# A two-layer transformer on one core: slot orders of three attention stages changed, start-up loads spread over the first stage

## The chip, the cores and the metric

The kernel runs on one core of a Trainium2 chip. The time is the device time of one execution in microseconds (us). TensorE (PE in the profile, PEld for its weight loads), VectorE (DVE), ScalarE (ACT), GpSimd (POOL) and SyncE (SP) run their own instruction streams and wait for each other by semaphores alone.

## The reference

`x` is 8 images of 256 tokens by 256 channels, float32. Eight sublayers run one after the other, each as `x = x + f(layernorm(x))`:

1. softmax attention, 16 heads of 16 channels (in the kernel: stage `attn_a0`, index A0S)
2. a linear layer with a scale per output row and a bias (`ffn0`, F1)
3. softmax attention over 4 wide heads of 64 channels, with biases (`attn_b0`, B0)
4. the linear layer of 2 again (`ffn0`, F3)
5. retention: scores times a decay mask `exp(-s*(t-k))`, two RMS norms, weights quantised to -1, 0, 1 (`ret1`, R1)
6. a gated feed-forward layer with a Hadamard transform (`ffn1`, F5)
7. differential attention **between the heads of one token**: 32 by 32 scores for each token, softmax, first half minus lambda times second half (`attn_b1`, B1)
8. the feed-forward layer of 6 again (`ffn1`, F7)

Matrix products of activations with weights are made to float32 precision from a high and a low part of each factor (three products); the retention's weights are exact in one part.

## The kernel before

All of `x` stays in SBUF. A stage handles one image in 8 slots of a global slot counter; `due(g, offset)` (L390) says that a step of image `b` falls in slot `8b + offset` of its stage. `together` (L420) walks the slots from -24 on and, in each, calls every stage's `at_slot(g)` on each engine. So each engine has one fixed order of instructions, written by hand: first by slot, then by stage, then by the order of the lines in that stage's `at_slot`. An engine that waits holds all that stands behind it. B0 begins at slot 76, F3 at 92, R1 at 148, F5 at 212, B1 at 276 and F7 at 338 (`START`, L417); F1 runs inside the slots of A0S. The stages overlap at their ends.

**Start (L470 to L495, L736 to L742, L881 to L889, L1240 to L1249, L2342 to L2344).** SP issues all input loads in one run: image 0 of `x`, the four `a0` weights, the identity matrix, small constants, images 1 to 7, more constants, the first raw weights (`f0`, `b0_q`, 1 MB of `w1`), the retention weights; only then does it reach the stage loops. Every progress semaphore begins at 1 rather than 0, so that a wait on image -1 passes: ACT increments each of them in a loop (L883 to L885), and DVE, POOL, SP and PE wait for `primed`, the last increment. POOL first fills constant rows of three K buffers, DVE fills four V buffers, and DVE splits all four `a0` weights into their low parts (`low_a0`) after the statistics of image 0. The one load semaphore of images 1 to 7 is waited for as a whole.

**Q and K in A0S and R1** go to DRAM (`store`, L506; four DMAs an image) and come back rearranged (`load_q`, `load_k`, L519 and L531; eight each). `pa` and `pb` are PSUM banks that x, Q, K and V outputs share.

**B0, one image (L2099 to L2121 on PE, L1501 to L1536 on DVE).** Slots 0 and 2: scores; DVE takes their maxima in 1 and 3. Slot 3: PE turns the next x and makes V (`v_out`, offset -5) into `pb`. Slot 4 on DVE: `x_low`, then `heads_out` of the second half (L1482: a reciprocal, a product), then far down the list `v_out` (L1461), which empties `pb`. Slot 4 on PE: `max_turned` (L2044) writes `pb`, and so waits for that `v_out`. Then K, the linear layer, transposed scores, `y_out`, Q.

**R1 (L1945 to L1967 on PE, L1379 to L1404 on DVE).** `k_out` of a later image stands in slot 5 (offset -11) and writes `pa`; it waits for `normed` of image b-3 (L1817), which DVE's `heads_out` of the second half makes in the same slot.

**B1 (L2204 to L2226 on PE, L1602 to L1622 on DVE, L1131 to L1157 on ACT).** Per image: `scores` of halves 0 and 1 (slots 0 and 1); DVE `less_maximum` (clamp, maximum, subtract; L1569), ACT `probs` (exp), DVE `weights_of` (sum, reciprocal, product; L1578), PE `turned` (slot 8), ACT `turned` (slot 8), PE `attend` (slot 9), ACT `heads_out` and `store_out` to DRAM, SP `load_out`, POOL `clipped`, ACT `squares`, DVE `square_sums` (slot 13), POOL `token_heads`, PE `a_turned` (18), `y_out` and DVE `residual` (24). PE's slot 0 holds, in order, `y_out` of image b-3, both `turned` of b-1, `x_turned` of b+2, and `scores(b, 0)`. ACT's slot 0 begins with `turned` of b-1.

Of the kernel before, what the change touches and what calls it, by code (L numbers as in the profile page):

```python
# [25 lines left out]
F32 = mybir.dt.float32  # L26
F32R = mybir.dt.float32r
ALU = mybir.AluOpType
# [3 lines left out]
P = 128  # L32
B = 8
# [104 lines left out]
class Signals:  # L138


    def __init__(self, ctx, nc):
# [4 lines left out]
        self.base, total = [], {k: 1 for k in names}  # L146
# [7 lines left out]
def build(nc, T, out):  # L154
    ctx = ExitStack()
    with ctx:
# [158 lines left out]
        x0_in, x_in, first_in, const_in = sem("x0_in"), sem("x_in"), sem("first_in"), sem("const_in")  # L315
        a0_in, a0_high, a0_low = sem("a0_in"), sem("a0_high"), sem("a0_low")
        negs_done, ones_done, k_ready, had_done = sem("negs_done"), sem("ones_done"), sem("k_ready"), sem("had_done")
        primed = sem("primed")
# [28 lines left out]
        A0 = ("a0_q", "a0_k", "a0_v", "a0_o")  # L347
        a0_raw = {n: prob_bufs[k // 2][:, k % 2 * 512:k % 2 * 512 + 512].rearrange("p (t n) -> p t n", t=CT) for k, n in enumerate(A0)}

        def split_done(eng, name):  # L350

            if name == "attn_a0":
                eng.wait_ge(a0_low, len(A0))
                return
            eng.wait_ge(w_split, ORDER.index(NEEDS[name]) + 1)


        def in_stage(eng, s, i):
# [10 lines left out]
            def prev(name, alone=apart):  # L369
                if name in per:  # L370
# [96 lines left out]
        n_const = 16 * (3 + 4 + 6 + 4)  # L467
# [3 lines left out]
        def _(sp):  # L471

            for b in range(B):
                sp.dma_start(x[:, b, :].rearrange("p (t c) -> p t c", t=TT),
                             T["hidden"][b].rearrange("(t p) c -> p t c", p=P)).then_inc(x_in if b else x0_in, 16)
                if b == 0:
                    for n in A0:
                        sp.dma_start(a0_raw[n], T[n].rearrange("(t p) n -> p t n", p=P)).then_inc(a0_in, 16)
                    for dst, src in ((ident[:], T["ident"]), (negs[:], T["r1_s"].rearrange("(a n) -> a n", a=1).to_broadcast([P, 16])),
                                     (diff[:], T["diff"])):  # L480
                        sp.dma_start(dst, src).then_inc(first_in, 16)
            for dst, src in ((caus[:], T["caus"]), (had_raw[:], T["had"]), (sel_raw, T["sel"])):
                sp.dma_start(dst, src).then_inc(const_in, 16)
            for dst, n in ((bq, "b0_bq"), (bk, "b0_bk"), (qkvn, "r1_qkvn"), (projn, "r1_projn")):
                sp.dma_start(dst[:], T[n]).then_inc(const_in, 16)
            for dst, n in ((bv[:], "b0_bv"), (bo0[:], "b0_bo"), (bo1[:], "b1_bo"), (bf[:], "f0_b"), (swb, "f0_s"), (nwb[:], "r1_nw")):
                sp.dma_start(dst, T[n].rearrange("(a n) -> a n", a=1).to_broadcast([P, C])).then_inc(const_in, 16)
# [1964 lines left out]
```

## Time and profile before

| | us |
|---|---|
| median of 3 runs | 1123.61 |
| the 3 runs | 1122.81, 1123.61, 1127.87 |
| the profiled execution | 1126.71 |
| its span, first to last instruction | 1124.9 |
| mean granted TensorE clock | 0.896 of full speed |

A row of the timeline gives the start in us from the span's start, the time, engine, line, operation, what is written from what, the count; in brackets the engine's idle time before it and what ended that. `SPq` and `ACTq` are DMA issues. A row of the waits gives total us, times, longest. In `--windows` rows the columns are the stretch, its length, and busy us (and instructions) of PE, PEld, DVE, ACT, POOL, then PE clock, DMA share and GB/s.

### The profile page before, as it was taken

What the parts mean: (1) busy time and instruction counts of PE and PEld (TensorE: products, weight loads), DVE (VectorE), ACT (ScalarE), POOL (GpSimd) and SP (SyncE); (2) the same over time, 40 slices, a digit from 0 to 9 for tenths busy, and PEclk for the clock granted to TensorE, in tenths of its full rate; (3) what the DMA queues carried; (4) which work ended last, traced back from release to release, by engine and by line L of the source; (5) the groups of instructions that cost most, each with busy time, mean ns of one, the idle gap of its engine ahead of it and who ended that gap; (6) DMA issues with size and microseconds to landing.
All of it is one profiled execution on the core that took longest, in us unless ns stands there. A gap on an engine that the chain in (4) does not pass through costs nothing.

```text
span 1124.9 us, 21059 instructions
## 1 busy us (share of the span) xinstructions
PE 915.9 (81%) x8018; PEld 776.4 (69%) x8018; DVE 695.5 (62%) x1291; ACT 367.3 (33%) x663; POOL 317.2 (28%) x352
## 2 busy tenths in 40 slices
PE   3589988787777678778877999997678874799998
PEld 2466665566666566656656999995566653799997
DVE  4468777646665567887775554536766767454443
ACT  2136554444222222233434332233222321332332
POOL 4202222224568474211111112100154443330000
PEclk9779998898898989898888999999777887899999
DMA  8745541001100002455440000022454445100000
GB/s 227 232 139 157 147 119 55 12 11 38 48 20 1 1 1 66 131 152 163 120 123 1 2 1 1 1 57 51 82 113 85 86 90 82 33 15 20 10 20 20
DMA packets 148580, 76.78 MB, mean 68 GB/s; under 512 B 108992, under 2 KB 139712, under 8 KB 148480
## 3 DMA queue, kind: packets, MB, share of 16 engines
q1 hardware_dynamic: 139376, 65.47, 23.1%
q0 software_dynamic: 1424, 4.98, 1.5%
q10 hardware_dynamic: 7680, 4.98, 1.5%
q8 instruction: 64, 1.05, 0.4%
q14 instruction: 36, 0.29, 0.1%
HBM read 45.77 MB, written 29.36 MB: 67 GB/s over the span
## 4 chain that ended last, share of the span: by engine, by line
PE 58%; DVE 26%; issue 7%; ACT 4%; SPq 2%; DMA 1%; POOL 1%; ACTq 0%; DVEq 0%; POOLq 0%
PE SC L380 17%; PE pb L380 8%; PE OT L380 8%; PE pa L380 4%; DVE mx L1315 3%; PE OT L2173 3%; PE OT L1890 3%; DVE OS L1488 2%; PE SC L1843 2%; PE SC L1872 2%; PE OT L2088 2%; PE SC L2161 2%; DVE pr L1576 2%; PE pa L2356 2%; DVE m L1574 2%
## 5 line engine op out<-in xcount | busy, mean ns | idle before, releaser
L380 PE MATMUL SC<-xT_h,w_h 128*128 128x256 f32 x512 | 148.3, 290 | 13.8 <-DVE xT_l L1737 11.5
L380 PE MATMUL SC<-xT_l,w_h 128*128 128x256 f32 x512 | 146.4, 286 | 0.0
L380 PE MATMUL SC<-xT_h,w_l 128*128 128x256 f32 x512 | 145.7, 285 | 0.0
L380 PEld LDWEIGHTS SC<-xT_h,w_h 128*128 128x128 f32 x512 | 98.4, 192 | 17.0 <-DVE xT_l L1737 15.1
L380 PE MATMUL OT<-w,Qs 128*128 128x256 f32 x768 | 102.9, 283 | 2.2 <-DVE Qs L1747 1.4
L1315 DVE TENSOR_REDUCE mx<-SC 128x4 f32<-128x1024 f32 x64 | 78.1, 1220 | 42.0 <-PE SC L1843 41.6
L380 PEld LDWEIGHTS SC<-xT_h,w_l 128*128 128x128 f32 x512 | 98.5, 192 | 0.0
L380 PEld LDWEIGHTS SC<-xT_l,w_h 128*128 128x128 f32 x512 | 98.2, 192 | 0.0
L380 PEld LDWEIGHTS OT<-w,Qs 128*128 128x128 f32 x768 | 95.1, 189 | 4.2 <-issue 2.6
L1743 DVE TENSOR_TENSOR hidden_f<-SC,silu_gate 128x512 f32<-128x512 f32 x64 | 44.1, 689 | 85.5 <-ACT silu_gate L1199 85.5
L1747 DVE TENSOR_TENSOR Qs<-hidden_f,Qs 128x512 fp32r<-128x512 f32 x64 | 45.2, 707 | 44.7 <-ACT Qs L1207 44.7
L1199 ACT ACTIVATE silu_gate<-SC 128x512 f32<-128x512 f32 x64 | 38.2, 597 | 101.5 <-PE SC L380 98.9
L749 POOL TENSOR_SCALAR ve<-mv 128x2 f32<-128x2 f32 x32 | 7.1, 221 | 191.3 <-DVE mv L1268 112.5
L1207 ACT ACTIVATE Qs<-hidden_f 128x512 fp32r<-128x512 f32 x64 | 40.4, 632 | 50.4 <-DVE hidden_f L1743 49.6
L2356 PE MATMUL pa<-ident,xn 128*128 128x128 f32 x192 | 34.0, 306 | 26.7 <-DVE xn L1291 20.3
L943 ACT ACTIVATE a_pr<-SC 128x1024 f32<-128x1024 f32 x32 | 32.8, 1026 | 49.2 <-PE SC L1872 49.2
L2356 PEld LDWEIGHTS pa<-ident,xn 128*128 128x128 f32 x192 | 24.4, 158 | 32.7 <-issue 21.3
L865 POOL TENSOR_SCALAR g_ve<-g_mv 128x2 f32<-128x2 f32 x16 | 3.9, 242 | 149.3 <-DVE g_mv L1722 148.8
L778 POOL TENSOR_TENSOR hr<-ssqe,half_pow 128x32 f32<-128x32 f32 x8 | 44.3, 5536 | 1.5 <-POOL ssqe L776 1.5
L943 ACT ACTIVATE pr<-SC 128x1024 f32<-128x1024 f32 x32 | 32.8, 1024 | 33.0 <-PE SC L1872 32.9
L764 POOL TENSOR_TENSOR x<-x,bo 128x512 f32<-128x512 f32 x16 | 20.4, 1273 | 67.9 <-DVE xn L1448 50.5
L1332 DVE TENSOR_TENSOR pr<-SC,mask 128x512 f32<-128x512 f32 x43 | 29.4, 685 | 16.2 <-PE SC L1872 15.9
(424 smaller groups left out, 2592.2 us busy)
## 6 DMA issues: line engine op xcount, KB each, us to landing
Qs<-q_stack SPq DMA_DIRECT2D x56, 128.0 KB, 2.8
k_stack<-KT_h SPq DMA_DIRECT2D x16, 256.0 KB, 2.4
k_stack<-KT_l SPq DMA_DIRECT2D x16, 256.0 KB, 3.1
q_stack<-QT_h SPq DMA_DIRECT2D x16, 256.0 KB, 2.2
q_stack<-QT_l SPq DMA_DIRECT2D x16, 256.0 KB, 2.8
o_groups<-b_O ACTq DMA_DIRECT2D x8, 512.0 KB, 3.0
Qs<-q_stack SPq DMA_DIRECT2D x56, 64.0 KB, 2.9
Ks<-k_stack SPq DMA_DIRECT2D x28, 128.0 KB, 3.0
```

Of the source, the lines that this page charges most:

```text
L380: ins = pe.matmul(out_ap, left[a], right[b], start=first and n == 0, stop=last and n == len(terms) - 1, **more)
L778: pool.tensor_tensor(hr0[:], ssqe[:], half_pow[:], ALU.pow).then_inc(sig.sem["hpow"], 1)
L943: act.activation(pr[(b * ROUNDS + r) % len(pr)][:], SC[1][:], ACT.Exp, scale=st.scale).then_inc(sig.sem["probs"], 1)
L1199: act.activation(silu_gate[:], SC[r % 2][:, 0:512], ACT.Silu).then_inc(sig.sem["g_silu"], 1)
L1207: act.activation(joined(hid[r % 2][0][:]), hidden_f[:], ACT.Copy).then_inc(sig.sem["g_hh"], 1)
L1315: dve.tensor_reduce(mx[:, t, m0:m0 + 16].rearrange("p (u g) -> p u g", u=2)[:, :, 2 * k:2 * k + 2], SC[0][:].rearrange("p (u g k) -> p u g ...
L1332: dve.tensor_tensor(to[:, :, 0, :], of[:, :, 0, :], heads, ALU.mult)
L1743: dve.tensor_tensor(hidden_f[:], SC[r % 2][:, 512:1024], silu_gate[:], ALU.mult).then_inc(sig.sem["g_hid"], 1)
L1747: dve.tensor_tensor(joined(hid[r % 2][1][:]), hidden_f[:], joined(hid[r % 2][0][:]).bitcast(F32), ALU.subtract)\
L1890: ins = pe.matmul(OT[0][32 * n:32 * n + 32, t0:S], Vr[b % len(Vr)][:, kt, 2 * r + u, :], p[:, u, kt, t0:S], start=kt == 0, stop=kt == 1, t ...
L2173: ins = pe.matmul(OT[0][:, 256 * h + 64 * n:256 * h + 64 * n + 64], b1_P[h][:, u, 8 * n:8 * n + 8, :].rearrange("p g b -> p (g b)"), own_h ...
L2356: ins = pe.transpose(ps[:, c * S + t * P:c * S + t * P + P], src[:, t, c * P:c * P + P], ident[:])
```

## The change

Six groups of edits, cut below to what matters.

- Semaphores count from 0, and a wait for 0 is left out; ACT's loop and `primed` go. ACT loads its function table with a small copy instead, then takes each `a0` weight as it lands.
- Each input has a semaphore of its own. SP first loads image 0, `a0_k`, the identity, `a0_q`, image 1, `a0_v`, image 2, `a0_o`. The other images and constants and weights are issued inside A0S's slots -2 to 50. The K fills are spread over POOL's slots, the four V fills stand behind `normalise` of images 0 and 1 on DVE, and `low_a0` is cut in two.
- The scale of `f0` has a semaphore of its own.
- B0: `v_out` of images 4 to 7 one slot earlier on PE, before `x_turned`; DVE's `v_out` right behind `maximum`; second `heads_out` and `a_low` one slot later.
- R1: K one slot later on all engines; `x_high` first in ACT's slot; `a_low` behind `masked` and `x_low`.
- B1: both `scores` first in slot 0; both `less_maximum` in slot 0; `weights_of` in slots 1 and 2; `probs` in 0 and 1, ahead of all else on ACT in slot 0, then `load_k` (six DMAs), then `turned`; `x_low` one slot later.

```diff
-        self.base, total = [], {k: 1 for k in names}
+        self.base, total = [], {k: 0 for k in names}
...
 # SP
+            X_LOADS = {-2: 3, 4: 4, 12: 5, 20: 6, 28: 7}
+            LATER = {1: 4, 3: 0, 5: 1, 6: 2, 7: 3, 11: 5, 36: 6, 44: 7, 46: 8, 48: 9, 50: 10}
+            load_x(0)
+            load_a0("a0_k")
+            sp.dma_start(ident[:], T["ident"]).then_inc(ident_in, 16)
+            load_a0("a0_q")
+            load_x(1)
+            load_a0("a0_v")
+            load_x(2)
+            load_a0("a0_o")
...
+                                if g in X_LOADS:
+                                    load_x(X_LOADS[g])
+                                if g in LATER:
+                                    load_later(LATER[g])
...
 # SP, ret1
-                                for b in due(g, -10):
+                                for b in due(g, -9):
                                     store(b, "kl", "kstore", "kload", KT, k_dram)
...
 # SP, attn_b1
+                            for b in due(g, -8):
+                                load_q(b)
                             for b in due(g, -7):
                                 load_k(b)
                             for b in due(g, 9):
                                 load_out(b)
-                            for b in due(g, -7):
-                                load_q(b)
...
 # POOL
+            clear_stack(0)
...
+                        if g in (-21, -13):
+                            clear_stack((g + 29) // 8)
...
 # ACT
-            for signal in sig.sem.values():
-                act.sem_inc(signal, 1)
-            act.sem_inc(primed, 1)
-
-            act.wait_ge(a0_in, 16 * len(A0))
+            act.wait_ge(ones_done, 1)
+            act.activation(silu_first[:], ones[:, 0:1], ACT.Copy)
             for n in A0:
+                act.wait_ge(a0_in[n], 16)
                 act.activation(W[n][0][:], a0_raw[n], ACT.Copy).then_inc(a0_high, 1)
...
 # ACT, attn_b1
+                    for b in due(g, 0):
+                        probs(b, 0)
+                    for b in due(g, -8):
+                        load_k(b)
                     for b in due(g, 8):
                         turned(b)
+                    for b in due(g, -16):
+                        high(b, x_pair(s, b), pa, "xT", "vp", 1, "xh")
+                    for b in due(g, 1):
+                        probs(b, 1)
                     for h in range(TT):
                         for b in due(g, 9):
                             heads_out(b, h)
-                    for b in due(g, 1):
-                        probs(b, 0)
                     for b in due(g, 9):
                         store_out(b)
...
 # DVE
+                    if s == 0 and b == 0:
+                        low_a0(1)
+                    if s == 0 and b < 2:
+                        for v in V_rings["attn_a0"][2 * b:2 * b + 2]:
+                            dve.memset(v[:], 1.0).then_inc(ones_done, 1)
...
 # DVE, attn_b0
+                    for b in due(g, -5):
+                        if b >= 4:
+                            v_out(b)
+                    for b in due(g, -4):
+                        if b < 4:
+                            v_out(b)
                     for b in due(g, 5):
                         max_low(b)
                     for b in due(g, -12):
                         x_low(b)
                     for c in range(CT):
-                        for b in due(g, 10 + 2 * c):
+                        for b in due(g, 10 + 3 * c):
                             heads_out(b, c)
-                    for b in due(g, 13):
+                    for b in due(g, 14):
                         a_low(b)
...
 # DVE, attn_b1
+                    for h in range(TT):
+                        for b in due(g, 0):
+                            less_maximum(b, h)
                     for b in due(g, 24):
                         residual(b)
-                    for b in due(g, -16):
+                    for b in due(g, 1):
+                        weights_of(b, 0)
+                    for b in due(g, -15):
                         low(b, x_pair(s, b), pa, "xh", "xl")
-                    for b in due(g, 1):
-                        less_maximum(b, 0)
                     for b in due(g, 2):
-                        weights_of(b, 0)
-                        less_maximum(b, 1)
+                        weights_of(b, 1)
...
-                    for b in due(g, 4):
-                        weights_of(b, 1)
...
 # PE, ret1
-                        for b in due(g, -11):
+                        for b in due(g, -10):
                             k_out(b)
...
 # PE, attn_b0
+                    for b in due(g, -6):
+                        if b >= 4:
+                            v_out(b)
                     for b in due(g, -13):
                         x_turned(b)
...
 # PE, attn_b1
+                    for h in range(TT):
+                        for b in due(g, 0):
+                            scores(b, h)
                     for b in due(g, 24):
                         y_out(b)
...
-                    for h in range(TT):
-                        for b in due(g, h):
-                            scores(b, h)
```

## Rows read from the trace of the kernel before

**Rows 1.** The page: the chain that ended last, by engine

```profile
PE 58%; DVE 26%; issue 7%; ACT 4%; SPq 2%; DMA 1%; POOL 1%; ACTq 0%; DVEq 0%; POOLq 0%
```

**Rows 2.** Windows: the start, B0, R1 and B1 in turn

```profile
0.00:40.30 40.30, 14.88 (x84) 13.37 (x84) 15.25 (x33) 8.63 (x14) 14.64 (x18) 0.96 0.82 235
...
250.00:429.00 179.00, 137.22 (x1192) 115.86 (x1186) 114.52 (x214) 45.91 (x85) 108.03 (x90) 0.90 0.05 17
...
465.00:600.00 135.00, 106.07 (x1048) 78.69 (x1048) 105.00 (x265) 48.26 (x137) 24.05 (x51) 0.87 0.45 131
...
769.00:968.00 199.00, 141.51 (x1292) 109.84 (x1291) 137.18 (x178) 53.48 (x78) 68.61 (x57) 0.78 0.45 81
```

**Rows 3.** Timeline of the start

```profile
0.91 3.65 POOL L738 MEMSET Ks<- 32x2048 f32 x2
1.15 0.91 DVE L1242 MEMSET V<- 128x1024 f32 x1 [0.16 <-issue]
...
8.55 0.75 DVE L1265 BATCH_NORM_STATS2 bst<-x 128x6 f32<-128x256 f32 x2 [3.27 <-ACTq L885]
...
17.79 0.58 PE L380 MATMUL pa<-xT_h,a_k_h 128*128 128x256 f32 x1 [1.41 <-DVE xT_l L1302]
...
24.34 0.55 SPq L512 DMA_DIRECT2D k_stack<-KT_h  x1
...
40.34 0.51 PE L1843 MATMUL SC<-Ks,Qs 48*128 48x256 f32 x4 [1.80 <-DMA Ks<-k_stack]
```

**Rows 4.** Issue to landing: all x loads, then all Q and K stores

```profile
DMA to landing us min/median/max: 2.8/5.2/6.7
...
DMA to landing us min/median/max: 2.1/2.8/7.9
```

**Rows 5.** Timeline of one B0 image

```profile
367.11 1.75 DVE L1488 RECIPROCAL OS<-OT 128x256 f32<-128x256 f32 x1
368.89 0.42 DVE L1490 TENSOR_TENSOR ON<-OT,OS 128x256 f32<-128x256 f32 x1
369.24 0.68 DVE L1466 TENSOR_TENSOR V<-pb,bv 128x512 f32<-128x512 f32 x1
...
370.06 0.66 PE L2050 MATMUL pb<-ident,sq 128*128 128x128 f32 x2 [4.28 <-DVE V L1466]
...
371.69 0.86 DVE L1494 TENSOR_TENSOR aT_l<-ON,aT_h 128x512 fp32r<-128x512 f32 x1
```

**Rows 6.** Waits in B0, 250 to 430 us

```profile
PE pb L2050 <- DVE V L1466: 17.2, 4, 4.4
...
PE pb L2050 <- DVE Vw L1466: 8.5, 3, 4.3
```

**Rows 7.** Waits in R1, 465 to 600 us

```profile
PE pa L380 <- DVE ON L1343: 5.5, 3, 2.3
...
PE pa L380 <- DVE scratch L1343: 3.9, 2, 2.3
```

**Rows 8.** Windows: the seven distances of DVE's first maximum in B1, together

```profile
sum 171.55, PE 128.25 PEld 101.53 DVE 119.78 ACT 45.56 POOL 58.30; mean PE 18.32 PEld 14.50 DVE 17.11 ACT 6.51 POOL 8.33
```

**Rows 9.** Timeline of one B1 image, and of the stage's end

```profile
848.35 1.92 PE L2188 MATMUL OT<-scratch,b_DT 128*32 128x128 f32 x64
...
852.37 1.06 ACT L1102 ACTIVATE pr<-pr 128x1024 f32<-128x1024 f32 x1 [1.43 <-DVE pr L1576]
...
854.10 2.19 ACTq L305 DMA_DIRECT2D b_KD<-k_tokens  x6
...
862.22 0.63 ACT L1116 ACTIVATE sq<-ON 128x512 f32<-128x512 f32 x1 [0.39 <-POOL ON L794]
...
864.68 3.51 PE L2173 MATMUL OT<-ident,V 128*128 128x64 f32 x16
...
944.47 1.23 DVE L1572 TENSOR_SCALAR pr<-SC 128x1024 f32<-128x1024 f32 x1 [3.07 <-PE SC L2161]
...
963.37 0.58 PE L380 MATMUL SC<-xT_h,w_h 128*128 128x256 f32 x1 [11.53 <-DVE xT_l L1737]
```

More of the change, by code:

```diff
@@ L369, in prev @@
             def prev(name, alone=apart):
-                if name in per:
+                if name in per and i * per[name] + base[name] > 0:
                     eng.wait_ge(sig.sem[name], i * per[name] + base[name])
@@ L471, in _, with load_x @@
         def _(sp):
-            for b in range(B):
+            def load_x(b):
                 sp.dma_start(x[:, b, :].rearrange("p (t c) -> p t c", t=TT),
[L475 to L481, printed above, removed]
@@ L1380, in at_slot @@
                     if ret:
-                        for b in due(g, 26):
-                            a_low(b)
                         for b, r in running(g, 0):
@@ L1386, in at_slot @@
                             x_low(b)
+                        for b in due(g, 26):
+                            a_low(b)
                         for b in due(g, -12):
                             low(b, QT, pb, "qh", "ql")
-                        for b in due(g, -10):
+                        for b in due(g, -9):
                             low(b, KT, pa, "kh", "kl")
@@ L1519, in at_slot @@
                         low(b, b0_Q, pb, "qh", bq, "ql")
-                    for b in due(g, -4):
-                        v_out(b)
                     for b in due(g, -21):
@@ L1808, in q_out @@
                     wait("al", b - 5, 1)
+                    if s == A0S and b == 0:
+                        pe.wait_ge(a0_low, 2)
                     if ret and b == 0:
@@ L1815, in k_out @@
                     wait("xl", b, 1)
+                    if s == A0S and b == 0:
+                        pe.wait_ge(a0_low, 1)
                     if ret:
@@ L1821, in v_out @@
                     wait("ql", b, 1)
+                    if s == A0S and b == 0:
+                        pe.wait_ge(a0_low, 3)
                     if s == A0S and b >= 6:
@@ L1963, in at_slot @@
                             q_out(b)
-                        for b in due(g, -11):
+                        for b in due(g, -10):
                             k_out(b)
@@ L2119, in at_slot @@
                     for b in due(g, -5):
-                        v_out(b)
+                        if b < 4:
+                            v_out(b)
                 return at_slot
```

105 lines of the change are left out of this document (57 added, 48 removed).

## The prediction

> **What bounds the kernel now.** First the page's chain: PE carries 58% of the chain that ended last and DVE 26% [rows 1], so most of the time PE works or DVE does while PE waits. Then the windows by stage [rows 2]: the feed-forward stages and the body of A0S, whose order the change leaves, are not among them; in the four stretches shown PE is busy for 37% of the start, 77% of B0, 79% of R1 and 71% of B1, and DVE for 38%, 64%, 78% and 69%. No engine is full there. The time goes into hand-overs within one fixed order per engine, so an edit of the order can move it. The reader should see in each of the next rows one such hand-over: an engine's idle time in brackets, and who ended it.
>
> **Start.** DVE has image 0 in SBUF 2.8 us after its issue at 0.7 (the shortest landing of its load [rows 4]), that is at 3.5, and begins its statistics at 8.55, released by ACT's loop of semaphore increments [rows 3]. That is 5.0 us of pure waiting, which counting from zero removes. What is late next: DVE must split the weights as they land (the last of them is issued at about 4.2, lands by the median of 5.2 us [rows 4] at 9.4, and two steps of the 128x512 kind, 0.63 us on ACT [rows 9] and put at 0.7 on DVE, split it by 10.7), and then two V fills stand ahead of `x_low` of image 0, each 0.91 us and a 0.16 gap [rows 3], 2.1 us, and `x_low` itself, 0.7. So the first K product starts at about 13.5 instead of 17.79 [rows 3]: 4.3 us. The K store now follows that product by 6.5 us (24.34 less 17.79), of which I estimate 2 us as SP still issuing loads (the product, two evictions and the issue make up the rest); that part goes too. The Q and K stores of image 0 then stand behind megabytes of weights: the slowest takes 7.9 us to land where the median of all is 2.8 [rows 4], 5.1 us more. Sum: 4.3 + 2 + 5.1 = 11. Given back: image 3 of `x` is now issued only in slot -2 behind the K fetch, and DVE's statistics of it stand in slot 1, in front of score maxima: I estimate 2 us from the landing time of 2.8 us; the second pair of V fills stands ahead of Q's low part of image 0, 1 us. **Term: -8 us**, ends -5 (only the removed loop) and -11.
>
> Costed at nothing: the K fills, now spread over POOL's slots (3.65 us each [rows 3], POOL being busy for 14.6 of the first 40.3 us [rows 2]; without that cover each would put 3.65 us ahead of a `rstd`); the table load, now under the first x load; the 31 later loads on SP, at about 0.45 us of issue each (a K store's took 0.55 [rows 3]) 14 us over 50 slots of more than 2 us, where SP mostly waits for PE and DVE (without that cover, see the third rival); the semaphore of `f0`'s scale, whose consumer is POOL slots later.
>
> **B0.** PE stands still before `max_turned` seven times, 17.2 + 8.5 = 25.7 us [rows 6]. Rows 5 show why: `pb` holds V until DVE's `v_out`, which waits its turn behind `x_low`, a 1.75 us reciprocal and a 0.42 us product, while PE idles 4.28 us. The change puts `v_out` ahead of these. The 2.2 us of reciprocal and product go one slot later, behind `max_low`; then `y_out` waits for them, for ACT's high part (0.6, as its square of that shape [rows 9]) and for `a_low` (0.86 [rows 5]). By the order of the slots PE meanwhile has the transposed max, K, the linear layer's turn and transposed scores to do, so I let about 1.1 us an image come back as a wait of `y_out`: 25.7 less 7 times 1.1. **Term: -18 us**, ends -10 (more comes back) and -26 (nothing does).
>
> **R1.** `k_out` waits in its slot for DVE's second `heads_out`: 5.5 + 3.9 = 9.4 us in five images [rows 7]. One slot later that work is done. But K then stands next to V in PE's order, in slots 6 and 7, and K's store and its fetch are one slot closer (3 us to land against two slots of 2 us). About half is kept. **Term: -5 us**, ends 0 and -9.
>
> **B1.** The seven distances between images are 171.55 us, 24.5 each, with 17.1 of DVE work in each [rows 8]. Now DVE ends an image's weights, PE turns both halves (3.51 us the first [rows 9]), turns an x, and only then makes the scores for which DVE waits (3.07 us idle at 944.47 [rows 9]). With `scores` first in PE's slot that wait goes. The next wait to end last is a longer one: on ACT, `turned` of image b-1 stands behind `probs(b, 0)` and six K issues. From DVE's first clamp T: clamp, maximum and subtract at 1.23 each (the clamp's row) 3.7, exp 1.06, six issues 2.19, an eviction 0.6 as the square of that shape [rows 9]: PE attends at T + 7.6. From there to the end of the squares now takes 14.5 us (848.35 to 862.85 [rows 9]: evictions, DRAM round trip, clip), 1.5 of it a queue on ACT that goes, so the squares end at T + 20.6. DVE's `square_sums` waits for them, then one `normalise`: the next T is 22 later, or a little more when PE runs at its lower level. I take 22.5 to 23 for six distances and 18.5 for the first, which has no such partner: 155 instead of 171.55. At the end 963.37 - 944.47 = 18.9 us pass from the last T to the feed-forward stage's first product [rows 9]; that product stands behind the squares of image 6, whose attend now falls about at T, so that they end some 15 us after it, and then 20.6: 5 to 6 are lost. **Term: 155 - 171.5 + 6 = -10 us**, ends -20 (distance 21.5, about DVE's 17.1 and its own waits) and +12 (26.5, with PE at the lower level and the ring as it stands).
>
> **Sum:** -8 - 18 - 5 - 10 = -41 us. The profiled execution took 1126.7 us, 1.8 over its span, which gives 1085.7; it stood 3.1 above the median of the runs, so a median of 1082.6, **1083 us**.
>
> **Rivals.** *B1 gives nothing* (0.15). For it: the round trip above is as long as the whole present distance, less 2 us. Against it: DVE's own work is 17.1 [rows 8], and part of the trip runs beside it. 1093 us.
>
> *B0 moves its wait* (0.12). PE's idle before `max_turned` goes, and the same time stands before `y_out`, because `heads_out`, ACT's high part and `a_low` are now the last link. For it: this chain is 2.2 + 0.6 + 0.9 us [rows 5, 9], nearly the 4.28 that goes. Against it: PE has work of about that length in between. 1101 us.
>
> *The loads in rounds push Q and K back* (0.08). Behind a run of weights the slowest store took 7.9 instead of 2.8 us [rows 4]; the loads left for the rounds are about 5.2 MB, at the 235 GB/s of the start [rows 2] 22 us of transfer, and if each one holds Q or K by its own length where PE waits for them, -8 becomes +14: 1105 us. The rows of a quiet queue speak against it: a Q or K fetch has a slot or more of slack. The Trainium skill ("DMA: Bandwidth & Descriptors", section "Queues, rings and completion order") says that each DMA engine consumes the descriptors of one issuer's ring in order; by that rule the rounds' loads delay whatever SP issues behind them, which would be this rival. The 7.9 us row agrees with the rule; whether PE then waits no run here shows.
>
> *Slower: DVE stands at `square_sums`* (0.07). Place: B1, DVE's slot 5. If the attend of image b-1 slips not only behind ACT's `probs` and issues but behind both of PE's turns at the lower clock level (7 us, by 3.51 a half [rows 9]), T to squares grows from 20.6 to some 28, and the distance to 30. Price: 7 times 5.5 is 39 us. It decides from a distance of 29 on (24.5 plus the other 31 us over seven). Then 1131 us.
>
> **How the numbers follow.** The forecast itself, all four terms with their sign, has 0.58. A change under 0.5% (5.6 us, about what a measurement of this kernel tells from none) needs two of the rivals together. Faster by more: the forecast, and nearly all of the first three rivals, 0.88; same 0.05; slower 0.07. The range: the terms' ends sum to -66 and +7; all at one end is unlikely, so it runs from 1060, nearly the lower sum, to 1112, past the third rival, and leaves out the fourth and the extremes.
>
> **What would show it.** In the changed profile: statistics at 3.5 us; first score product near 31 us instead of 40.34; no PE wait on DVE's V before `max_turned`, at most 1 to 2 us before `y_out`, and B0 some 18 us shorter; no `pa` wait on `heads_out` in R1; in B1 clamps 22 to 23 us apart, DVE idle before `square_sums`, not before the clamp. Wrong would be: clamps over 25 apart, a Q or K fetch ending PE's waits in the first stage, or `y_out` waiting 4 us in B0.

## The result and the profile after

The changed kernel takes 1091.83 us (median of 4 runs, 1081.66 to 1093.77), the kernel before 1123.21 in the same comparison: a ratio of 0.9697, 95% interval 0.9628 to 0.9766, so 3.0% less. (The ratio, here and below, is taken over the runs; the two medians alone give 0.9721.) Ratios are of fast runs alone, which leaves out one run of e1 below (2039.78 us), one of e9 (1088.25 us), and two or three runs of the kernel before beside e5 to e8 and beside e12 (1136.72 to 1143.41 us). The profiled execution took 1093.38 us with a span of 1091.6.

Marks in the two traces tell where the time went. A stage's mark is the start of an instruction that each image has once or in a known number: DVE's first score maximum (A0S, B0), its first masked product (R1), its first maximum of the clamped scores (B1, 1.25 us behind the first clamp, so with the same distances). R1 ends with its last masked product, F5 with its last SiLU. Marks are rounded to 0.1 us.

| stretch, us | before | after | difference | forecast |
|---|---|---|---|---|
| span's start to A0S's first maximum | 40.9 | 36.3 | -4.6 | -11 of the start term |
| A0S, first to last image | 145.4 | 154.6 | +9.2 | +3 of the start term |
| A0S's last to B0's first | 66.0 | 62.1 | -3.9 | 0 |
| B0, first to last image | 173.9 | 157.3 | -16.6 | -18 |
| B0's last to R1's first | 38.2 | 43.8 | +5.6 | 0 |
| R1, first image to its end | 136.1 | 131.2 | -4.9 | -5 |
| F5's end to B1's first | 8.8 | 4.5 | -4.3 | 0 |
| B1, first to last image | 171.6 | 155.0 | -16.6 | -16.5 |
| B1's last to F7's first SiLU | 22.4 | 24.9 | +2.5 | +6 |

The distances of B0 and B1 and R1's stretch came out within 2 us of their numbers. The start did not: up to the first maximum it gains less than half of what was forecast, and the distances from image 0 to image 2 then lose almost twice that (8.5 of the 9.2 us; the table of first maxima below has them).

The page's part 4 of the changed kernel, the chain that ended last by engine, is to be read against [rows 1]. PE and DVE have shrunk, and DMA has grown from 1% to 5%. By line, 4 of these 5% are the two legs of B1's trip through DRAM (`DMA o_groups<-b_O` 2%, `DMA ON<-o_groups` 2%).

```profile
PE 52%; DVE 23%; issue 8%; DMA 5%; ACT 4%; SPq 3%; POOL 3%; ACTq 1%; POOLq 0%; DVEq 0%
```

**The start.** The timeline of the changed kernel (start, busy us, engine, line, tiles, in brackets the idle time before and who ended it):

```profile
3.46 0.75 DVE L1293 BATCH_NORM_STATS2 bst<-x 128x6 f32<-128x256 f32 x2 [2.47 <-DMA x<-in_hidden]
...
6.48 3.69 POOL L765 MEMSET a_K<- 32x2048 f32 x2 [0.15 <-POOL rstd L778]
7.53 2.79 DVE L1319 TENSOR_SCALAR xn<-x,mv,rstd 128x256 f32<-128x256 f32 x2
...
11.96 0.91 DVE L1325 MEMSET V<- 128x1024 f32 x1 [0.16 <-issue]
13.04 0.91 DVE L1325 MEMSET a_V<- 128x1024 f32 x1 [0.16 <-issue]
...
14.55 0.58 PE L380 MATMUL pa<-xT_h,a_k_h 128*128 128x256 f32 x1 [3.00 <-DVE xT_l L1335]
...
18.75 2.28 DVE L1319 TENSOR_SCALAR xn<-x,mv,rstd 128x256 f32<-128x256 f32 x2
18.93 0.37 SPq L533 DMA_DIRECT2D k_stack<-KT_h  x1
...
21.20 0.91 DVE L1325 MEMSET a_V<- 128x1024 f32 x1 [0.16 <-issue]
22.27 0.91 DVE L1325 MEMSET a_V<- 128x1024 f32 x1 [0.16 <-issue]
23.82 0.36 SPq L533 DMA_DIRECT2D q_stack<-QT_h  x1
...
35.72 0.51 PE L1886 MATMUL SC<-Ks,Qs 48*128 48x256 f32 x4
```

Statistics begin at 3.46 and the first K product at 14.55, close to the forecast (3.5 and 13.5). But DVE normalises image 0 in 2.79 us and image 1 in 2.28, while POOL fills a K stack (L765), and between K's store (18.93) and Q's (23.82) lie 4.9 us, in which DVE does that slow pair and two V fills. So the first score product is at 35.72 instead of the forecast 31.

Behind it, two waits of the changed kernel, from the waits of PE and of DVE (34 to 108 us; columns: us in total, times, longest), neither of which the kernel before has:

```profile
PE SC L1915 <- DMA Qs<-MT_l: 3.5, 1, 3.5
```
```profile
DVE bst L1293 <- DMA x<-in_hidden: 3.1, 1, 3.1
```

DVE stands 3.1 us for image 3 of `x`; at PE the transposed scores stand 3.5 us for the maxima's rows. The view of the fetch line, 63 to 73 us, shows the queue in which those rows travel: the fetches of image 2 take 6.8 us to land, where the median of the line over the whole trace is 3.0. They were issued right behind nine constant loads (59.1 to 63.4 us).

```profile
DMA to landing us min/median/max: 3.8/6.8/6.9
```

These waits are not the whole loss. The windows from image 1's first maximum to image 2's, before and after (PE busy and count first; the granted clock is the number after POOL's):

```profile
62.20:81.90 19.70, 15.14 (x112) 11.30 (x110) 13.25 (x18) 6.36 (x10) 0.94 (x2) 0.74 0.44 136
```
```profile
59.30:85.80 26.50, 19.12 (x110) 14.56 (x110) 13.36 (x18) 6.93 (x11) 0.94 (x2) 0.62 0.73 154
```

Nearly the same products take PE 4 us longer at a lower granted clock, so more of this stretch ran at the lower of TensorE's two levels (1.2 and 2.4 GHz). What part of the 6.8 us that costs the image, and whether the waits are what lowers the clock, no run here separates.

**B0.** PE's waits, 250 to 412 us, against [rows 6]:

```profile
PE pb L380 <- DVE aT_l L1527: 10.9, 6, 3.1
...
PE pb L2095 <- DVE Vw L1499: 2.3, 1, 2.3
PE pb L2095 <- DVE V L1499: 1.9, 3, 0.9
```

The 25.7 us before `max_turned` (there L2050, here L2095) are 4.2. The new wait is the one named beforehand, `y_out` for `aT_l`: 1.8 us in each of six images where I let 1.1 come back.

**R1.** PE's waits, 452 to 585 us, against [rows 7]: no `pa` wait on `heads_out` is left. PE waits longer for DVE's masked products instead, 18.1 us by two lines where the same view of the kernel before (465 to 600 us, shown first) has 11.6: 6.5 of the 9.4 us come back there, somewhat more than the half of the forecast. By the mark the stage is 4.9 us shorter. One trace doesn't fix the size: in the ten traces here with this order the stretch takes from 124.3 to 131.2 us, in the four without it (before, e2, e3, e4) from 133.5 to 136.1.

```profile
PE OT L1890 <- DVE pr L1333: 7.7, 11, 1.5
...
PE OT L1890 <- DVE r_pr L1333: 3.9, 6, 1.0
```
```profile
PE OT L1933 <- DVE pr L1366: 12.3, 13, 1.6
PE OT L1933 <- DVE r_pr L1366: 5.8, 7, 1.4
```

**B1.** DVE's longest wait before (769 to 968 us), then its waits after (753 to 934 us) and the windows of the seven distances together, against [rows 8]:

```profile
DVE pr L1572 <- PE SC L2161: 19.1, 8, 7.1
```
```profile
DVE ssq L1632 <- ACT sq L1147: 33.1, 7, 6.4
DVE xn L1593 <- POOL rstd L778: 5.9, 5, 1.3
DVE pr L1609 <- PE SC L2210: 2.1, 1, 2.1
```
```profile
sum 155.00, PE 116.39 PEld 92.83 DVE 114.60 ACT 45.81 POOL 57.85; mean PE 16.63 PEld 13.26 DVE 16.37 ACT 6.54 POOL 8.26
```

DVE's wait for scores falls from 19.1 to 2.1 us; it now waits in every image for the squares. The distances are 22.1 us in the mean, with 16.4 of DVE's own work. The round trip has the length of the forecast: the sums of squares below start 20.7 us behind the clamp at 863.38, where the forecast had T + 20.6, and the next clamp follows at 884.72.

```profile
884.12 0.69 DVE L1632 TENSOR_REDUCE ssq<-sq 128x32 f32<-128x512 f32 x1 [5.41 <-ACT sq L1147]
```

### The profile page after: what moved, and what is told of

Same layout as the page of the kernel before. It is cut to its first block, busy times and chain, and to the rows that moved or that the text cites. A ratio compares the mean times of both kernels' runs of the same rounds, so it can differ in the third digit from the quotient of the medians.

```text
span 1091.6 us, 20960 instructions
## 1 busy us (share of the span) xinstructions
PE 902.0 (83%) x8018; PEld 766.6 (70%) x8018; DVE 695.2 (64%) x1291; ACT 367.4 (34%) x664; POOL 320.3 (29%) x352
## 4 chain that ended last, share of the span: by engine, by line
PE 52%; DVE 23%; issue 8%; DMA 5%; ACT 4%; SPq 3%; POOL 3%; ACTq 1%; POOLq 0%; DVEq 0%
PE SC L380 17%; PE pb L380 8%; PE OT L380 8%; PE pa L380 3%; PE OT L1933 3%; DVE mx L1348 3%; PE SC L1915 2%; DVE OS L1521 2%; DMA ON<-o_groups 2%; PE OT L2237 2%; PE OT L2133 2%; PE SC L1886 2%; DMA o_groups<-b_O 2%; PE pa L2404 1%; SPq L644 1%
## 5 line engine op out<-in xcount | busy, mean ns | idle before, releaser
L1230 ACT ACTIVATE silu_gate<-SC 128x512 f32<-128x512 f32 x64 | 38.2, 597 | 96.9 <-PE SC L380 96.4
L2237 PE MATMUL OT<-scratch,b_DT 128*32 128x128 f32 x512 | 24.8, 375 | 29.4 <-ACT b_DT L1138 29.4
L2404 PE MATMUL pa<-ident,xn 128*128 128x128 f32 x192 | 32.7, 297 | 17.6 <-DVE xn L1319 13.0
L2237 PEld LDWEIGHTS OT<-scratch,b_DT 128*32 128x32 f32 x512 | 22.4, 155 | 30.8 <-issue 30.7
```

The source lines that it names most:

```text
L1230: act.activation(silu_gate[:], SC[r % 2][:, 0:512], ACT.Silu).then_inc(sig.sem["g_silu"], 1)
L2237: ins = pe.matmul(OT[h][32 * i:32 * i + 32, P * n:P * n + P], b1_DT[:, 4 * h + n, a0:a0 + 32], b1_VB[:, 8 * i + 4 * h + n].rearrange("p e ...
L2404: ins = pe.transpose(ps[:, c * S + t * P:c * S + t * P + P], src[:, t, c * P:c * P + P], ident[:])
```

## Experiments

The theory after the result: the three orders do what was forecast, and the changed start does not, for causes of its own. The kernel before measures 1123 us in the first comparison and 1129 to 1137 on the later chips, so kernels are compared by their ratio to it.

### One part at a time

e1 is the kernel before with the three changed orders, e2 with the changed start alone, e3 and e4 with B0's and B1's order alone. Each takes the hunks of the diff above that belong to its part, for example all of e3 on DVE:

```diff
+                    for b in due(g, -5):
+                        if b >= 4:
+                            v_out(b)
+                    for b in due(g, -4):
+                        if b < 4:
+                            v_out(b)
...
-                        for b in due(g, 10 + 2 * c):
+                        for b in due(g, 10 + 3 * c):
...
-                    for b in due(g, 13):
+                    for b in due(g, 14):
                         a_low(b)
...
-                    for b in due(g, -4):
-                        v_out(b)
```

> Kernel before with the changed orders of B0, R1 and B1, and its own start. Theory A (the start term failed: by the stage marks of the two traces the changed start gains 4.6 us up to the first score maximum and gives back 9.2 over images 0 to 2): 1123 - 38 = 1085 us, some 5 us below the changed kernel's 1092. Rival B (the start is worth its -8 and one of the orders brought less than its stage marks say): 1100 us. By the spread of the runs so far (12 us in the changed kernel) a difference of 5 us is at the edge of what can be told.

> Kernel before with the changed start alone (counts from zero, a semaphore per input, loads in rounds). Theory A: 1123 + 4.6 = 1128 us; the first score maximum near 36.3 us instead of 40.9, the last of the stage near 191 instead of 186. Rival B: 1115 us, the last maximum of the stage near 178.

> Kernel before with the changed order of B0 alone. Theory A (the seven distances shrink by 16.6 and the 5.6 us that were lost between B0's last maximum and R1's first mask come from R1's order): 1106 us. Rival B (those 5.6 us are B0's own, work that its last images push behind them): 1112 us.

> Kernel before with the changed order of B1 alone. Theory A (seven distances -16.6, lead-in -4.3, tail +2.5): 1123 - 18.4 = 1105 us, clamps 22 us apart with DVE waiting at square_sums. Rival B (part of that is the earlier stages' doing, the clock level that they leave): 1111 us or more.

| kernel | ratio to before | 95% interval |
|---|---|---|
| e1, three orders | 0.9634 | 0.9601 to 0.9666 |
| e2, start | 1.0008 | 0.9977 to 1.0039 |
| e3, B0 | 0.9836 | 0.9805 to 0.9868 |
| e4, B1 | 0.9833 | 0.9803 to 0.9862 |

Of 1128.7 us (the kernel before in this set) B0's order takes 18.5 and B1's 18.8; what is left of e1's 41.3 us, 4, would be R1's, less than the intervals of the three ratios can tell from nothing (R1's order wasn't run alone). e1 and e4 come out as their theories A, reckoned from 1128.7: 1087.1 us against 1091, and 1109.0 against 1110, with rivals at 1106 and 1117. e3 falls between its two cases as worded in us, but those were reckoned from 1123; from 1128.7, A means 1111 and B 1117, and 1109.7 speaks for A on the time. In its trace, though, B0's last maximum to R1's first mask is 42.9 us against 38.2, so 4.7 of the 5.6 us do come with B0's order; its distances shrink by 18.2 and R1 behind it by 2.6, and from B0's first maximum to R1's end the trace is 16.1 us shorter.

The start alone is worth nothing: neither A's +4.6 nor B's -8 is in the time. Its marks are A's all the same (first maximum 36.2, last 190.6). But of the 4.3 us by which the stage ends late, 2 are the spread of single traces: e1, e3 and e4, which keep the start of the kernel before, end it at 188.1 to 188.3 and not at 186.3. The rest is made up behind it, by image 2 of B0 (301.6 against 301.7 before). The windows of e2 from A0S's last maximum to B0's first and on to its third show how (PE busy and count first, then the other engines; the granted clock is the number after POOL's):

```profile
190.60:254.10 63.50, 49.82 (x464) 34.70 (x461) 38.40 (x91) 30.78 (x49) 19.91 (x26) 0.92 0.06 15
254.10:301.60 47.50, 36.39 (x318) 32.12 (x318) 30.95 (x59) 17.20 (x36) 25.61 (x21) 0.89 0.09 28
```

and the same of e4, whose code up to B1 is that of the kernel before:

```profile
188.30:252.80 64.50, 51.95 (x464) 35.87 (x463) 38.44 (x90) 30.78 (x49) 19.72 (x25) 0.88 0.05 14
252.80:303.40 50.60, 39.49 (x319) 34.66 (x319) 31.02 (x60) 17.33 (x36) 25.74 (x21) 0.83 0.09 27
```

The same 464 instructions of the first window take PE 49.8 us at a granted clock of 0.92 and 52.0 at 0.88. PE ran at its upper level (2.4 GHz) for more of this stretch in e2. One profile of each doesn't settle whether the changed start brings that about, but other traces speak for executions that differ: from A0S's last maximum to B0's first, e4 takes 64.5 us where the kernel before, the same code up to there, takes 66.1, and e10 takes 66.2 where e8, again the same code up to there, takes 62.1. So the -3.9 us of that row in the table of marks need not be a gain of the change. What is measured is the sum, nothing.

### What the start lost

e5, e6 and e7 each mend one suspect of the changed kernel:

```diff
-                    item(pool, A0S, "rstd", n - 1, 1)
+                    item(pool, A0S, "xn", n - 1, TT)
```
```diff
-            X_LOADS = {-2: 3, 4: 4, 12: 5, 20: 6, 28: 7}
+            X_LOADS = {-2: 4, 4: 5, 12: 6, 20: 7}
...
             load_a0("a0_o")
+            load_x(3)
```
```diff
-            LATER = {1: 4, 3: 0, 5: 1, 6: 2, 7: 3, 11: 5, 36: 6, 44: 7, 46: 8, 48: 9, 50: 10}
+            LATER = {1: 4, 11: 5, 13: 0, 15: 1, 17: 2, 19: 3, 36: 6, 44: 7, 46: 8, 48: 9, 50: 10}
```

> Changed kernel; POOL fills the K stacks of images 1 and 2 after DVE has normalised image 0 and 1, instead of beside it. Theory A (a pair of 128x256 tensor_scalar on DVE stands still while POOL's fill runs): the pairs take 0.73 us each instead of 2.79 and 2.28, the first score maximum is at 33 to 34 us instead of 36.3, the stage's last at 187 to 189 instead of 190.9. Rival B (the pair is slow for another reason, the loads that write x at that time): it still takes over 2 us, nothing moves.

> Changed kernel; image 3 of x is loaded ahead of the slots and each later image one round earlier. Theory A: DVE's wait of 3.09 us for image 3 and PE's 2.84 behind it go; the distance from image 0's first maximum to image 1's is 20 us instead of 23.0, the last maximum of the stage 2 to 3 us earlier (188). Rival B (256 KB more ahead of image 0's K and Q stores): the first maximum is over 1 us later, the last where it was.

> Changed kernel; the four groups of constants move from slots 3 to 7 to slots 13 to 19. Theory A (the Q and K fetches of images 1 and 2 stand behind them on SP and in its DMA queue): fetches land in about 3 us instead of 6.8, the distances of the first two images fall from 23.0 and 26.5 us to 20 or 21 each, the last maximum of the stage 6 to 8 us earlier, 183 to 185. Rival B (they hold up whatever is behind them, wherever they are): the first two distances fall, and the third to fifth grow from 17.6, 19.3 and 22.9 by as much; the last maximum stays at 190. Rival C (the low granted clock of these images, 0.62 to 0.70, makes them long): no distance falls by more than 1 us.

> Changed kernel with the three edits (fills after normalise, image 3 early, constants in slots 13 to 19) and the V fills two slots later, where DVE waits for ACT. Theory A: first maximum near 31 us, last of the stage near 177, and the time by 10 us or more below the changed kernel's, 1078 to 1082 us by the runs so far. Rival B (what the start loses or gains up to here is taken back by the stages behind it, as with the changed start alone, whose last maximum was 4.3 us late and whose time was the same): the last maximum is early, and the time within 4 us of the kernel before with the changed orders alone, 1083 to 1089.

First maxima of the eight images in A0S, by the traces:

| kernel | first | distances | last | ratio to before (interval) |
|---|---|---|---|---|
| before | 40.9 | 21.4, 19.7, 17.6, 19.3, 22.9, 22.4, 22.2 | 186.3 | 1 |
| changed | 36.3 | 23.1, 26.5, 17.6, 19.3, 22.9, 22.4, 22.9 | 190.9 | 0.9697 (0.9628 to 0.9766) |
| e5, fills after normalise | 33.4 | 23.4, 26.5, 17.6, 19.3, 22.9, 22.4, 22.8 | 188.3 | 0.9651 (0.9576 to 0.9725) |
| e6, image 3 early | 36.6 | 21.6, 24.9, 17.6, 19.3, 22.8, 22.4, 22.8 | 188.0 | 0.9618 (0.9556 to 0.9679) |
| e7, constants in slots 13 to 19 | 35.9 | 23.2, 23.4, 17.6, 23.4, 22.9, 22.4, 24.0 | 192.9 | 0.9705 (0.9639 to 0.9771) |
| e8, all three and the V fills | 27.8 | 18.0, 19.7, 19.3, 25.1, 22.9, 22.4, 23.0 | 178.2 | 0.9563 (0.9508 to 0.9618) |

The ratios of e5, e6 and e7 don't differ from the changed kernel's clear of their intervals, so these three are judged by rows and marks alone.

**e5** settles its question. Its timeline, against that of the changed kernel above:

```profile
7.72 0.73 DVE L1319 TENSOR_SCALAR xn<-x,mv,rstd 128x256 f32<-128x256 f32 x2
8.61 3.65 POOL L765 MEMSET a_K<- 32x2048 f32 x2 [2.29 <-DVE xn L1319]
...
17.73 0.73 DVE L1319 TENSOR_SCALAR xn<-x,mv,rstd 128x256 f32<-128x256 f32 x2
18.61 3.66 POOL L765 MEMSET a_K<- 32x2048 f32 x2 [2.89 <-DVE xn L1319]
18.61 0.91 DVE L1325 MEMSET a_V<- 128x1024 f32 x1 [0.16 <-issue]
```

The same pairs take 0.73 us once POOL's fill is not running, and the stage starts 2.9 us and ends 2.7 us earlier, as theory A had it. It was the fill. Not every operation of DVE suffers from it: the V fill beside the second K fill takes its usual 0.91. The Trainium skill ("SBUF — State Buffer", section "Who interferes with whom") says that VectorE and GpSimd share one pair of SBUF ports under an exclusive lock, that `tensor_scalar` can take it where a `tensor_reduce` cannot, and that whoever comes second stands still until the first is done. By that rule the pair waits for the fill, and the rows agree: of image 0's pair the second instruction alone takes 1.97 us (the row below), and the pair ends 0.15 us behind POOL's fills (7.53 + 2.79 against 6.48 + 3.69).

```profile
8.35 1.97 DVE L1319 TENSOR_SCALAR xn<-x,mv,rstd 128x256 f32<-128x256 f32 x1
```

**e6** gains 2.9 us at the stage's end, as expected, and DVE's wait for image 3 is gone from its list, though the first distance falls by 1.5 rather than 3; the other half falls in the second.

**e7** shows rival B at work beside A. The second distance falls by 3.1 us (forecast 6) and the first not at all, and the fourth grows by 4.1. Rival C fails as worded, since one distance fell by over 1 us; but PE still takes 18.9 us in the second at a granted clock of 0.56, so the clock may hold the rest. In the fourth PE waits

```profile
PE SC L1915 <- DMA a_Q<-MT_l: 2.5, 1, 2.5
```

and the stores of that image (the view of L533, 93 to 101 us), issued behind the broadcast constants, take up to 6.7 us to land, where the changed kernel's take 3.4 to 4.3 at that place:

```profile
DMA to landing us min/median/max: 4.0/5.4/6.7
```

In both places the constants cost their place in SP's queue. The Trainium skill's rule of the prediction ("DMA: Bandwidth & Descriptors", section "Queues, rings and completion order": on each DMA engine one issuer's descriptors are consumed in order) agrees with that.

**e8** also moves the V fills, two to DVE's place behind the statistics of image 1 and two behind those of image 2, where DVE waited 2.7 us for ACT (L1339, K's low part). Its start:

```profile
15.93 0.37 SPq L534 DMA_DIRECT2D k_stack<-KT_h  x1
...
17.68 0.36 SPq L534 DMA_DIRECT2D q_stack<-QT_h  x1
...
27.29 0.51 PE L1887 MATMUL SC<-Ks,Qs 48*128 48x256 f32 x4
```

Q's store now follows K's by 1.8 us instead of 4.9, and the first score product is at 27.3, earlier than the forecast 31. The first maximum is 5.6 us ahead of e5's. The V fills weren't tried alone, so that share is by difference, and the clock has a part in it: up to the first maximum PE's 88 products take 16.8 us in e5 at a granted clock of 0.90 and 14.0 in e8 at 1.00.

```profile
0.00:33.36 33.36, 16.84 (x88) 15.17 (x88) 15.19 (x34) 8.35 (x14) 14.18 (x17) 0.90 0.44 139
```
```profile
0.00:27.84 27.84, 13.98 (x88) 12.23 (x88) 15.16 (x34) 8.35 (x14) 14.10 (x17) 1.00 0.54 170
```

The stage ends at 178.2 (A: 177), and the ratio is 0.0071 below that of e1, some 8 us. The two intervals overlap by a little, so e8 alone doesn't show that the gain of the start reaches the end, against rival B; e9 below, whose interval lies clear of e1's, does. In the traces e8 and e9 are both some 12 us ahead of e1 at B1's first maximum.

### Where constants have cover, and what sets B1's distance

e9 is e8 with the constants in slots 40 to 53 (`bf` alone, which POOL needs earlier, in slot 22 with a semaphore of its own). e10 is e8 with the squares' sums of B1 three slots later, e11 both edits, e12 is e9 with the sums two slots later, behind stats and normalise:

```diff
-            LATER = {1: 4, 11: 5, 13: 0, 15: 1, 17: 2, 19: 3, 36: 6, 44: 7, 46: 8, 48: 9, 50: 10}
+            LATER = {1: 4, 11: 5, 22: 11, 40: 2, 49: 0, 51: 1, 53: 3, 36: 6, 44: 7, 46: 8, 48: 9, 50: 10}
```
```diff
 # DVE, behind both less_maximum
+                    for b in due(g, 16):
+                        square_sums(b)
...
-                    for b in due(g, 13):
-                        square_sums(b)
...
 # POOL
-                    for b in due(g, 13):
+                    for b in due(g, 16):
                         token_heads(b)
```
```diff
-                    for b in due(g, 13):
-                        square_sums(b)
                     for b in due(g, -20):
                         stats(b)
                     for b in due(g, -17):
                         normalise(b)
+                    for b in due(g, 15):
+                        square_sums(b)
```

> As e8_start_mended, but the constants, bf apart, move on to slots 40 to 53, the last images. In e7 and e8 the groups in slots 13 to 19 made the distance from image 3's first maximum to image 4's 23.4 and 25.2 us instead of 19.3 (stores behind them landed in 5.5 to 6.7 us). Theory A (late in the stage, where an image has 22.9 us of PE's and DVE's own work, a load has cover): that distance falls to 19 or 20, none of the later ones grows by over 1 us, the last maximum at 173 to 174 instead of 178.2, the time 3 to 5 us below e8's. Rival B (they cost their place in the queue wherever they stand): one of the last three distances is 3 to 5 us longer, the last maximum at 177 to 179, the time as e8's.

> As e8_start_mended, with DVE's square_sums and POOL's token_heads of B1 three slots later (slot 16, behind the next image's clamps). Theory A (B1's distance is the round trip from clamp to squares, where DVE waits 33.1 us in seven images): clamps 19 to 20.5 us apart instead of 22.1, the seven distances 133 to 144 us instead of 155, the stage's end later by 2 to 6, the time by 7 to 16 us below e8's. Rival B (PE's attend, which waits 29.4 us for ACT's turned blocks, is the limit): clamps still 22 apart, PE's wait for ACT as long, the time as e8's or up to 6 us above it.

> The edits of e9 and e10 together on e8. Theory A of both: their gains add, 1062 to 1074 us where e8 is at 1082 (12 to 16 below it at best). Rival: what e10 saves in B1 comes back as a lower granted clock in the stages behind, and the sum is less than the parts by 4 us or more.

> As e9_consts_late, with DVE's square_sums of B1 moved behind stats and normalise (slot 15 instead of 13); POOL's order stays, so that nothing waits longer for token_heads than it does. Theory A (the distance is the round trip from clamp to squares plus what DVE does between the squares and the next clamp): in the five distances that have a normalise (22.1 to 23.4 us in the changed kernel, 21.3 to 23.4 in e9) 1 to 1.8 us go, all seven sum to 147 to 150 us instead of 153.6, the time by 4 to 7 us below e9's. Rival B (the next clamp waits for the scores, or normalise, now ahead, waits for POOL's rstd as long as before while nothing else moves): the seven distances stay within 1.5 us of 153.6, and the time is e9's.

| kernel | ratio to before | 95% interval | B1's seven distances, us |
|---|---|---|---|
| e9 | 0.9468 | 0.9409 to 0.9527 | 153.6 |
| e8, for comparison | 0.9563 | 0.9508 to 0.9618 | 159.3 |
| e10 | 0.9769 | 0.9721 to 0.9818 | 166.5 |
| e11 | 0.9692 | 0.9650 to 0.9735 | 166.7 |
| e12 | 0.9527 | 0.9457 to 0.9598 | 156.7 |

The last column needs its spread: with one and the same order of B1 the seven distances sum to 152.5 (e1) to 159.3 us (e8) in the traces of the changed kernel, e1 and e4 to e9.

**e9**: the distance behind image 3 is 19.3 us again, the later ones are 22.9, 22.4 and 23.5, and the stage ends at 175.2, 3.0 earlier than e8's (expected 4 to 5; its first maximum and two first distances came out longer than e8's, for a cause that no run shows). No wait of PE on the maxima's rows is left in the stage.

Other traces with the same code up to B1 bear on this. The distance behind image 3 is 25.1 us in e8 and 24.9 in e10, and 19.3 in e9, e11 and e12: what the move takes away there is repeated. The cover late in the stage isn't complete: in e12 all late distances are under 23.3 us, but in e11 one is 25.9 where e9 has 22.4, at a granted clock of 0.87 instead of 1.00, and PE waits 1.5 us for the maxima's rows in it. The stage ends at 178.2 and 180.8 with the old places, and at 175.2, 176.9 and 172.4 with the new ones.

The ratio of e9 is 0.0095 below e8's, more than 3 us would make, and the intervals overlap; in the two traces the 3 us are gone by B1's first maximum (737.0 against 736.3), and e9's B1, the same code, is some 6 us shorter. That the constants bring the whole 1% is not shown. e9's ratio is the lowest of all, 1074.27 us where the kernel before takes 1135.01; e12's (1074.11 against 1136.52) can't be told from it.

**e10** answered neither way, and by the ratios it is some 23 us slower than e8. PE's waits, 740 to 960 us:

```profile
PE OT L2405 <- POOL ON L814: 45.4, 6, 8.5
...
PE OT L2238 <- ACT b_DT L1139: 7.8, 7, 3.6
```

PE's turn of the heads, two slots behind the sums' new place, stands up to 8.5 us for POOL, whose `token_heads` I moved too. The slots between the two had been cover for POOL's work, and the edit spent it. DVE's wait at the squares is gone from its list, and PE's for ACT fell to 7.8 us (29.9 in e8), but behind a new and longer wait neither says what limited the distance before. **e11** repeats it: its distances are e10's. Its ratio is 0.0077 below e10's, of the size of the step from e8 to e9, though these two intervals overlap as well.

**e12** leaves POOL's place alone. DVE's waits, 733 to 912 us, in e9 and then in e12:

```profile
DVE ssq L1638 <- ACT sq L1153: 32.7, 7, 6.3
DVE xn L1599 <- POOL rstd L782: 5.8, 5, 1.3
```
```profile
DVE xn L1599 <- POOL rstd L782: 27.1, 5, 6.9
DVE ssq L1638 <- ACT sq L1153: 11.4, 2, 5.8
```

The wait has changed its name and not its length: 38.5 us in the two lines where e9 has 38.5 (32.7 for the squares and 5.8 for `rstd`). POOL's timeline says why:

```profile
812.14 0.61 POOL L825 TENSOR_SCALAR ON<-ON 128x512 f32<-128x512 f32 x1 [10.71 <-DMA ON<-o_groups]
812.73 1.28 POOL L795 TENSOR_TENSOR x<-x,bo 128x512 f32<-128x512 f32 x1
814.09 0.23 POOL L780 TENSOR_SCALAR ve<-mv 128x2 f32<-128x2 f32 x1
814.50 0.72 POOL L782 TENSOR_TENSOR rstd<-ve,half_pow 128x2 f32<-128x2 f32 x1 [0.18 <-POOL ve L780]
```

`rstd`, for which normalise waits, stands on POOL behind the clip, and the clip waits for the outputs' trip through DRAM. Squares and normalise hang on the same trip: two of DVE's steps depend on its end, and POOL's order ties the second to it. That is the mechanism of e12's rival B. Its number is not met to the letter, 156.7 being 3.1 above e9's where 1.5 was allowed, but that lies within the spread above, and the time is e9's. That the round trip sets B1's distance is told by these waits, by the page's chain and by its length; an edit that takes `rstd` out from behind the clip, and so would shorten the distance, was not run.

## Why the prediction was right, and where it was not

- **The total** (forecast 1083 us, measured 1091.83) stands partly by luck, because two of its terms missed in opposite directions. The three orders were put at -33 together and bring -41 (e1); the start was put at -8 and brings 0 (e2), and in company with the orders perhaps a loss: the changed kernel's ratio is 0.0063 above e1's, about 7 us, with intervals that overlap.
- **Start, the term that failed.** The removed loop is worth its 5.0 us (statistics at 3.46), and Q's and K's stores of image 0 land in 2.1 to 2.5 us instead of up to 7.9. Three steps were wrong. "Costed at nothing: the K fills, now spread over POOL's slots": their price isn't on POOL but on DVE, 2.06 and 1.55 us of normalise, 2.7 us at the stage's end (e5). "Given back: image 3 ... 2 us": 2.9 (e6). "The 31 later loads on SP ... where SP mostly waits": not the issue costs but the queue behind it; the constants in slots 3 to 7 cost image 1's distance 3.1 us (e7), and in slots 40 to 53, where an image has its own 22.9 us of work, no more than 0.6 in e9, but 3.5 in one distance of e11, a part of it with a lower clock. The V fills' 2.1 + 1 us were in the forecast, but as a cost to be borne; they stand ahead of both stores, and moving them brings 5.6 us by difference, of which PE's clock may hold 2.9. The lower clock in image 1's distance, 4 us of PE's time, is in no term, and its cause stays open.
- **The rival "loads in rounds push Q and K back"** (0.08) is what happened in part. Its price of +22 us, the bytes of all loads, was the wrong measure: where a cost was found it was that of the few loads directly ahead of a needed transfer, 3 to 4 us a group. The transfer that PE waited for was not a Q or K fetch but the maxima's rows.
- **B0** was right in mechanism, place and size: -16.6 by the marks, -18.5 by e3. The wait that comes back is the named one, 1.8 us an image instead of 1.1. Not foreseen is the longer way to R1, +4.7 in e3.
- **R1** was right in mechanism and place: the waits on `heads_out` are gone and about two thirds of them come back. Its size is only known roughly, -4.9 by the marks and -4 by difference in the runs, each with a spread as large.
- **B1** was right in its distance (22.1 against 22.5 to 23, sum 155.0 against 155) and in what ends it, DVE at `square_sums`, right ahead of normalise and the next clamp. Mis-sized is the rest of the term: the end loses 2.5 us instead of 6, and the lead-in, not in the sum, gains 4.3. That gain comes with B1's order (F5's end to B1's first is 8.9 us in e2 and e3 and 4.6 in e1 and e4); that it is due to `scores` and the clamp standing first in their slots is likely and not shown. So -18.8 (e4) and not -10. The slower rival, attend behind both of PE's turns, did not come: DVE's wait for squares is 6.4 us at its longest, and PE's for ACT's blocks 29.4 us in all.
- **The range** rests on a wrong sum: the upper ends of the four terms, -5, -10, 0 and +12, add up to -3 and not to +7. Its upper bound of 1112 us came from the third rival and did not depend on it.

## What to carry to other kernels

An edit of a fixed order can be priced from the trace: find the wait that goes, then the chain that ends next, and work out its length from durations; all three orders came out so in place and cause, and the two experiments that moved one more step (e10, e12) failed where that second chain wasn't followed through every engine's queue. Work that is "hidden on an idle engine" or "hidden on a queue" is only free if nothing that is needed soon shares its port or stands behind it: see what runs beside it and what is issued after it, and put it where the neighbours have work of their own to spare. A start-up gain should be followed through the next images before it is added to a sum, and a mark of one trace compared with the same mark in other traces of the same code.

## What was not expected of the hardware

- A pair of 128x256 `tensor_scalar` on DVE took 2.79 and 2.28 us beside a POOL fill of 32x2048 and 0.73 without it (e5), and the fill itself 3.69 against 3.65: here DVE bears it alone.
- Behind a group of broadcast constants, transfers of 64 to 256 KB, whose medians over the trace are 2.8 (stores) and 3.0 us (fetches), took 5.4 (stores, e7) and 6.8 us (fetches, the changed kernel).
- A stage that ended 2 to 4 us late left no trace in the time (e2), with a granted clock of 0.92 and 0.89 behind it where another execution of the same instructions had 0.88 and 0.83. The same code took 62.1 and 66.2 us ahead of B0 (e8, e10), and from 152.5 to 159.3 in B1. A mark in one profile can't be booked as a gain or loss of the whole without the runs.
